# A graph network kernel with another prologue: loads in order of use, groups' columns side by side, small groups' second products turned, graph 0's norm and sums beside layer 0

## The chip, the cores and the metric

The kernel runs on one core of a Trainium2 chip. The metric is the device time of one execution in microseconds (us). Three runs of the kernel before took 2833.07, 2834.61 and 2835.61 us; the median is 2834.61.

## The reference

Four layers run one after another over 16 graphs of 1024 nodes with 256 features each; after each layer the input is added and the row is normalised (mean and variance over the 256 features). `A` is a dense 1024 x 1024 adjacency per graph.

```python
x = layernorm(x + L0(x, adj))     # layer 0: only the first 25 nodes of a graph
x = layernorm(x + L1(x, adj))     # layer 1: attention, z = x W^T + bW, softmax(leaky(ai + aj^T) masked by adj > 0) @ z
x = layernorm(x + L2(x, adj))     # layer 2: relu(((1 + eps) x + adj @ x) @ W1 + b1) @ W2 + b2
x = layernorm(x + L3(x, adj))     # layer 3: silu(rmsnorm((eps x + adj @ x) @ W1 + b1) * w) @ W2 + b2

# layer 0, for five groups of nodes: all 25; 0-8; 0 and 9-14; 6-8 and 12-14; 3-5 and 9-11
A = adj_g + I;  d = rowsum(A) ** -0.5;  N = d[:, None] * A * d[None, :]
h   = relu(N @ (x_g @ W1[g]) + b1[g])          # 256 -> 512
o_g = relu(N @ (h   @ W2[g]) + b2[g])          # 512 -> 256
fused[group] += softmax(fusion_w)[g] * o_g
```

Only the first 25 rows of each graph are changed by layer 0 before its norm; the other rows are normalised as they come in.

## The kernel before

The program has two blocks. **prologue** makes everything that all graphs share, and layer 0 of all 16 graphs; **layers** then runs layers 1 to 3 graph by graph. Each block gives every engine a queue written out by hand: `sp` (SyncE, loads and stores), `act` (ScalarE), `pool` (GpSimd), `dve` (VectorE) and `pe` (TensorE). An engine works its queue in order and waits on semaphores (`wait_ge`); the next block begins when all engines have left the one before. In the profile, SPq and ACTq are the issues of loads on the queues of SyncE and ScalarE.

**Prologue.** Four graphs of 32 padded rows fill the 128 partitions, so layer 0 has T0 = 4 tiles of rows. SP waits for two memsets, then issues 32 small loads (L155 and L157: for each graph the 25 x 25 corner of the adjacency into `A0` and 25 rows into `X0`), then the group weights `G1` and `G2` (L158, L159) and the weights of layers 2 and 3 (L160 to L163). ScalarE issues W_nat (L174) and 16 small columns and rows (L177, L195). VectorE waits for all 15 columns, builds the row mask and a zeroed copy of A, waits for the 32 loads, adds the identity (L278), copies the groups' blocks (L282), sums rows (L285); POOL raises them to -1/2 (L244); VectorE scales A (L292). It then waits for all five weights and splits W12, W13 and W23 into a high and a low part (L297, L298), so that fp32 products can be made of three faster ones. TensorE begins only when all weights and columns are there (L370, then L376, L382, L388), then transposes A (L395, five banks); VectorE scales these into `AT` (L333). TensorE multiplies x with A's columns: for each group, half of the features, tile and run of nodes one product (L410, 64 of them, 4 to 100 columns wide), and VectorE copies each bank to `XaT` (L338). In the profile an fp32 product is recorded as two instructions, a transpose as one.

For each group g, `hidden(g)` makes x A W1 (L427, eight products), ScalarE adds the bias and takes the relu into `H1` (L213, one instruction a run of nodes, four graphs' rows padded to 32). Then the second product takes H1 as weights, four tiles of 128 padded rows by G2 (L442, 16 products of 256 columns), VectorE copies to `Z` (L344), TensorE multiplies by AT (L447, four products), VectorE adds the bias (L349), ScalarE takes the relu scaled by the fusion weight (L227), POOL adds it to X0 (L250). The group's steps follow one another; only hidden(g + 1) is made ahead. At the end SP waits for all additions, stores the 16 graphs' 25 rows to `x_l0` (L168), and waits for the stores.

**Layers.** `load_x` (L620 to L623) and `load_row` (L626) bring graph 0's x and adjacency. VectorE takes statistics (L1347, L1351, L1355), POOL the inverse root (L1177), VectorE normalises (L1362) and makes two weighted sums of each row (`attention_sums`, L1370) that give `ai` and `aj` (L1376, L1377). TensorE spreads aj along rows (L732); VectorE and ScalarE make scores, mask, maximum and exponential (L1383, L1012, L1389, L1394, L1017). Then `turn_att` (L705) transposes the attention, two banks for a tile of 1024 columns; ScalarE casts each bank to the high part (L965), VectorE makes the low part (L1301) and so frees the bank. All eight tiles are turned, and then the aggregation of layer 1, first half of the columns, runs (`agg_step`, L754, L755, L758: six products of 512 columns per step, eight steps). Each step frees a tile of the adjacency's columns for a load (L644). For later graphs all this is woven into the graph before. `graph(b, first)` on TensorE then turns the adjacency's columns (`turn_col`, L719): in the first graph six of them ahead of the second half of the aggregation, the others by `COL_AT` between its steps. The rest of a graph (layers 2 and 3) is the same for every graph.

```python
for k in range(NT):                       # TensorE, graph 0, before
    turn_att(0, k)
...
for k in range(6):
    turn_col(b, k, 0)
for k in range(NT):
    agg_step(b, 1, k, 1)
    if k in COL_AT:
        turn_col(b, *COL_AT[k])
    if k == 2:
        attention_out(b, 0, first)
```

## Time and profile before

| | us |
|---|---|
| median of 3 runs | 2834.61 |
| lowest and highest | 2833.07, 2835.61 |
| profiled execution, its own time | 2838.37 |
| its span, first to last instruction | 2836.6 |
| TensorE busy (matmul) | 2685.7 (95%) |
| VectorE busy | 2027.3 (71%) |
| ScalarE busy | 1561.6 (55%) |
| POOL busy | 1273.3 (45%) |
| mean granted TensorE clock | 0.98 of full speed |

### The profile page before, as it was taken

What the parts mean: (1) busy time and instruction counts of PE and PEld (TensorE: products, weight loads), DVE (VectorE), ACT (ScalarE), POOL (GpSimd) and SP (SyncE); (2) the same over time, 40 slices, a digit from 0 to 9 for tenths busy, and PEclk for the clock granted to TensorE, in tenths of its full rate; (3) what the DMA queues carried; (4) which work ended last, traced back from release to release, by engine and by line L of the source; (5) the groups of instructions that cost most, each with busy time, mean ns of one, the idle gap of its engine ahead of it and who ended that gap; (6) DMA issues with size and microseconds to landing.
All of it is one profiled execution on the core that took longest, in us unless ns stands there. A gap on an engine that the chain in (4) does not pass through costs nothing.

```text
span 2836.6 us, 41497 instructions
## 1 busy us (share of the span) xinstructions
PE 2685.7 (95%) x14794; PEld 2292.9 (81%) x14794; DVE 2027.3 (71%) x4517; ACT 1561.6 (55%) x2900; POOL 1273.3 (45%) x1392
## 2 busy tenths in 40 slices
PE   3928999999999999999999999999999999999997
PEld 3717888888888888888888888888888888888886
DVE  4256687786868678686868778686867868686735
ACT  0233665756475665656466575647556565746624
POOL 1113455453545455354545545354555535454532
PEclk9959999999999999999999999999999999999999
DMA  4024030220404021130403022040402113040200
GB/s 144 1 80 134 1 119 31 70 79 8 142 1 149 1 86 64 32 118 1 149 1 118 32 72 78 7 143 1 149 1 86 64 32 118 1 149 1 75 1 15
DMA packets 205501, 181.06 MB, mean 64 GB/s; under 512 B 17616, under 2 KB 186992, under 8 KB 205296
## 3 DMA queue, kind: packets, MB, share of 16 engines
q1 hardware_dynamic: 197728, 177.06, 19.4%
q10 hardware_dynamic: 7568, 1.34, 0.3%
q8 instruction: 119, 1.95, 0.3%
q14 instruction: 86, 0.70, 0.1%
HBM read 161.17 MB, written 17.19 MB: 63 GB/s over the span
## 4 chain that ended last, share of the span: by engine, by line
PE 67%; DVE 15%; ACT 7%; issue 3%; POOL 1%; DMA 1%; SPq 0%; ACTq 0%; DVEq 0%; POOLq 0%
PE bank L754 9%; PE bank L758 9%; PE bank L755 9%; PE bank L819 8%; PE bank L804 6%; PE bank L809 6%; PE bank L805 6%; PE bank L833 5%; PE bank L705 4%; DVE stat L1347 3%; PE bank L837 3%; DVE x_odd L1362 2%; DVE x_even L1362 2%; DVE hid L1431 2%; PE bank L719 2%
## 5 line engine op out<-in xcount | busy, mean ns | idle before, releaser
L754 PE MATMUL bank<-mt_hi,x_hi 128*128 128x512 f32 x1536 | 629.1, 410 | 0.0
L758 PE MATMUL bank<-mt_hi,x_lo 128*128 128x512 f32 x1536 | 602.6, 392 | 0.0
L755 PE MATMUL bank<-mt_lo,x_hi 128*128 128x512 f32 x1536 | 599.7, 390 | 0.0
L1177 POOL TENSOR_TENSOR rstd<-ve,neg_half 128x4 f32<-128x4 f32 x128 | 164.1, 1282 | 437.0 <-DVE ve L1355 435.4
L758 PEld LDWEIGHTS bank<-mt_hi,x_lo 128*128 128x128 f32 x1536 | 288.8, 188 | 63.7
L754 PEld LDWEIGHTS bank<-mt_hi,x_hi 128*128 128x128 f32 x1536 | 289.6, 189 | 53.7 <-ACT scratch L1048 4.2
L755 PEld LDWEIGHTS bank<-mt_lo,x_hi 128*128 128x128 f32 x1536 | 290.2, 189 | 50.8
L804 PE MATMUL bank<-a_hi,W_lo 128*128 128x512 f32 x768 | 319.5, 416 | 1.7
L1415 DVE TENSOR_TENSOR sq_sum<-sq_sum,scratch 128x512 f32<-128x512 f32 x224 | 154.8, 691 | 227.3 <-ACT scratch L1048 227.3
L805 PE MATMUL bank<-a_hi,W_hi 128*128 128x512 f32 x768 | 303.3, 395 | 0.0
L976 ACT ACTIVATE mt_hi<-bank 128x512 fp32r<-128x512 f32 x256 | 153.4, 599 | 243.9 <-PE bank L719 243.9
L833 PE MATMUL bank<-W_hi,hid_hi 128*128 128x256 f32 x1024 | 260.5, 288 | 17.3 <-ACT hid_hi L1058 17.3
L1039 ACT ACTIVATE hid<-bank,b 128x512 f32<-128x512 f32 x256 | 176.4, 689 | 140.5 <-PE bank L837 83.5
L833 PE MATMUL bank<-W_lo,hid_hi 128*128 128x256 f32 x1024 | 252.4, 280 | 0.0
L1319 DVE TENSOR_TENSOR a_lo<-bank,a_hi 128x512 fp32r<-128x512 f32 x192 | 126.3, 686 | 176.3 <-ACT a_hi L993 176.2
L809 PE MATMUL bank<-a_lo,W_hi 128*128 128x512 f32 x768 | 241.7, 396 | 0.0
L1053 ACT ACTIVATE hid<-hid 128x512 f32<-128x512 f32 x256 | 161.6, 631 | 145.3 <-DVE hid L1431 143.6
L1182 POOL TENSOR_TENSOR x_lo<-x_even,x_hi 128x256 fp32r<-128x256 f32 x192 | 163.3, 866 | 154.1 <-ACT x_hi L1003 154.1
L993 ACT ACTIVATE a_hi<-bank 128x512 fp32r<-128x512 f32 x192 | 109.3, 594 | 217.2 <-PE bank L758 212.5
L819 PE MATMUL bank<-W,hid 128*128 128x256 f32 x1024 | 226.2, 379 | 0.0
L1307 DVE TENSOR_TENSOR mt_lo<-bank,mt_hi 128x512 fp32r<-128x512 f32 x256 | 173.1, 686 | 70.2 <-ACT mt_hi L976 70.2
L1182 POOL TENSOR_TENSOR x_lo<-x_odd,x_hi 128x256 fp32r<-128x256 f32 x192 | 161.9, 858 | 125.0 <-ACT x_hi L1003 125.0
(147 smaller groups left out, 6153.8 us busy)
## 6 DMA issues: line engine op xcount, KB each, us to landing
att<-in_adj SPq DMA_DIRECT2D x128, 512.0 KB, 7.8
adj_col<-in_adj SPq DMA_DIRECT2D x256, 256.0 KB, 3.0
out<-x_even SPq DMA_DIRECT2D x64, 128.0 KB, 2.9
out<-x_odd SPq DMA_DIRECT2D x64, 128.0 KB, 2.8
x_even<-in_x SPq DMA_DIRECT2D x56, 128.0 KB, 4.7
x_odd<-in_x SPq DMA_DIRECT2D x56, 128.0 KB, 3.6
G<-in_L_gnn_W SPq DMA_DIRECT2D x2, 2560.0 KB, 13.5
W_f<-in_L_gnn_W SPq DMA_DIRECT2D x1, 1024.0 KB, 9.1
```

What stands on the lines that cost most here:

```text
L754: nc.tensor.matmul(dst[:], hi, mt_hi[:, k, cols], start=k == 0, stop=False)
L755: nc.tensor.matmul(dst[:], hi, mt_lo[:, k, cols], start=False, stop=False)
L758: mm = nc.tensor.matmul(dst[:], lo, mt_hi[:, k, cols], start=False, stop=done)
L804: nc.tensor.matmul(dst, w_lo[:, d, cols], a_hi[:, d, :], start=d == 0, stop=False)
L805: nc.tensor.matmul(dst, w_hi[:, d, cols], a_hi[:, d, :], start=False, stop=False)
L809: mm = nc.tensor.matmul(dst, w_hi[:, d, cols], a_lo[:, d, :], start=False, stop=d == DT - 1)
L819: mm = nc.tensor.matmul(out_bank[t // 2][:, t % 2 * D:(t % 2 + 1) * D], src[:, t * P:(t + 1) * P], W22[:, m, :], start=(m == 0 and t % 2 = ...
L833: nc.tensor.matmul(out_bank[t // 2][:, t % 2 * D:(t % 2 + 1) * D], hi[:, t * P:(t + 1) * P], r[:, m, :], start=(m == 0 and t % 2 == 0 and ...
L1039: nc.scalar.activation(hid[:, m, :], src, ACT.Identity, bias=b13[:, m:m + 1])
L1177: nc.gpsimd.tensor_tensor(rstd[:, norm, own], ve[:, norm, own], neg_half[:, 0:4], ALU.pow)\
L1182: nc.gpsimd.tensor_tensor(x_lo[:, t, :], x_bufs[buf][:, t, :], x_hi[:, t, :].bitcast(F32), ALU.subtract).then_inc(s_x_lo, 1)
L1307: nc.vector.tensor_tensor(mt_lo[:, k, cols], turn_bank[i][:], mt_hi[:, k, cols].bitcast(F32), ALU.subtract).then_inc(s_turn_free[i], 1)
```

## The change

1. **Loads.** Layer 0's 32 small loads become eight: for each of the four positions i in a tile, one load brings the corners (or rows) of all four tiles. G1 and G2 come in two parts, group 0 first. Then follow graph 0's x straight into `x_even` (all rows but the first 25), W12, W13, W23, W22, and graph 0's eight adjacency rows into `att`. ScalarE's small loads come in order of use and have semaphores of their own, so that TensorE's first products wait for four loads, VectorE for five scalars. The raw W12, W13 and W23 lie where their low parts go.
2. **Order.** VectorE's memsets come ahead of its waits. WT's split and the scaled identities are made while POOL takes the power. W12 and W13 are split on VectorE after graph 0's statistics; W23's high part is made on ScalarE and its low part on POOL.
3. **Columns side by side.** ScalarE copies the five groups' columns of AT without padding into `AT_side` (212 columns a tile; 32 copies). Eight products of 212 columns, two to a bank, replace the 64 of L410, and four copies replace ten.
4. **Second products.** Group 0 keeps its form. For groups 1 to 4, `second_rows` takes W2's columns as weights and the unpadded hidden rows (144, 112, 96, 96 wide) as the moving side, eight products; VectorE copies them to `ZT` with padding, `second` transposes ZT back (eight transposes), VectorE copies to `Z`. Z, Ot, Or and the additions are now pairs of tiles, 512 columns. The groups overlap more: hidden(g + 2) is made before outputs(g).
5. **Graph 0.** Its statistics, norm and attention sums stand in VectorE's queue among the groups, tile 0 last, when layer 0 has been added. ai and aj are made in the prologue; the block layers starts with aj_rows. Four stores replace 16, and nothing of graph 0 is read back.
6. **First graph's turns.** Two tiles are turned ahead; tile k + 2 is turned before step k of the first aggregation. The columns are turned behind the steps of the second half (`FIRST_COL_AT`). SP's wait for the norm of graph 0 ahead of the column loads is gone.

```diff
                 sp.wait_ge(s_zero, 2)
-                for b in range(GRAPHS):
-                    t, i = b // PER, b % PER
+                for i in range(PER):
                     rows = slice(PAD * i, PAD * i + L0_NODES)
-                    sp.dma_start(A0[rows, 0, b, 0:L0_NODES],
-                                 adj[b, 0:L0_NODES, 0:L0_NODES]).then_inc(s_aload, 16)
-                    sp.dma_start(X0[rows, t, :], x[b, 0:L0_NODES, :]).then_inc(s_aload, 16)
+                    blocks = A0[rows, 0].rearrange("p (t i) j -> p t i j", i=PER)[:, :, i, 0:L0_NODES]
+                    own = adj.rearrange("(t i) n m -> i n t m", i=PER)[i]
+                    sp.dma_start(blocks, own[0:L0_NODES, :, 0:L0_NODES]).then_inc(s_aload, 16)
+                for i in range(PER):
+                    rows = slice(PAD * i, PAD * i + L0_NODES)
+                    own = x.rearrange("(t i) n d -> i n t d", i=PER)[i]
+                    sp.dma_start(X0[rows, :, :], own[0:L0_NODES]).then_inc(s_aload, 16)
...
+                for t in range(NT):
+                    sp.dma_start(att[:, t, :], adj[0, t * P:(t + 1) * P, :]).then_inc(s_att_in[t], 16)
...
+                for g in range(3):
+                    hidden_rows(g)
+                    if g == 2:
+                        act.wait_ge(s_wload, 16 * 4)
+                        nc.scalar.activation(W23_hi[:], W23[:], ACT.Copy).then_inc(s_w23, 1)
+                for g in range(NG):
+                    group_relu(g)
+                    if g + 3 < NG:
+                        hidden_rows(g + 3)
...
+                rstd_of(REST, 0)
+                pool.wait_ge(s_w23, 1)
+                nc.gpsimd.tensor_tensor(W23_lo[:], W23[:], W23_hi[:].bitcast(F32), ALU.subtract)
+                for i in range(NG * PAIRS):
                     pool.wait_ge(s_or, i + 1)
...
+                x_statistics()
+                split(W12, W12_hi, W12_lo)
+                split(W13, W13_hi, W13_lo)
+                dve.wait_ge(s_gbload, 32)
+                second(0)
+                second_rows(1)
+                x_norm(range(1, NT), 1)
+                outputs(0)
+                second(1)
+                second_rows(2)
+                attention_sums(range(1, 5), NT - 1)
+                outputs(1)
+                second(2)
+                second_rows(3)
+                attention_sums(range(5, NT), NT - 1)
+                outputs(2)
+                second(3)
+                second_rows(4)
+                outputs(3)
+                second(4)
+                outputs(4)
...
+                hidden(0)
+                hidden(1)
+                second(0)
+                second_rows(1)
                 for g in range(NG):
+                    if g + 2 < NG:
+                        hidden(g + 2)
+                    outputs(g)
                     if g + 1 < NG:
-                        h = hidden(g + 1, h)
...
+                        second(g + 1)
+                    if g + 2 < NG:
+                        second_rows(g + 2)
...
+    FIRST_COL_AT = ((0,), (1,), (2,), (3,), (4,), (5,), (6, 7), (8, 9, 10))
...
                     turned(turn_att_use(b, k))
+                    if first and k + 2 < NT:
+                        turn_att(b, k + 2)
                     agg_step(b, 1, k, 0, None if first or k else (s_sq, b * 2 * HT3))
```

## Rows read from the trace of the kernel before

**Rows 1.** Stretches: start:end and length in us, busy us by engine, clock, DMA share, GB/s.

```profile
16.60:41.70 25.10, 0.00 (x0) 0.01 (x1) 11.09 (x30) 0.39 (x2) 3.55 (x1) 1.00 0.97 351
41.70:55.30 13.60, 12.72 (x50) 11.59 (x51) 13.32 (x20) 0.00 (x0) 0.00 (x0) 1.00 0.00 1
55.30:79.40 24.10, 24.10 (x130) 24.10 (x129) 4.61 (x12) 0.00 (x0) 0.00 (x0) 0.62 0.00 1
79.40:150.30 70.90, 61.43 (x281) 49.42 (x281) 17.25 (x41) 18.87 (x52) 14.05 (x20) 0.96 0.00 1
150.30:180.40 30.10, 0.00 (x0) 0.00 (x0) 13.65 (x60) 0.00 (x0) 2.32 (x3) 0.50 0.52 188
202.65:232.50 29.85, 25.27 (x113) 19.95 (x113) 11.85 (x19) 12.36 (x25) 7.67 (x12) 0.74 0.18 54
232.50:260.50 28.00, 22.27 (x115) 18.20 (x114) 16.93 (x43) 11.84 (x29) 9.21 (x13) 0.88 0.55 176
380.00:542.00 162.00, 160.75 (x898) 137.38 (x897) 124.21 (x276) 96.35 (x179) 78.66 (x85) 1.00 0.21 66
```

**Rows 2.** Timeline, 0 to 52 us: start, length, engine, line, instruction, idle before.

```profile
15.90 0.30 SPq L157 DMA_DIRECT2D X<-in_x  x1
...
21.10 0.90 DVE L278 TENSOR_TENSOR A<-A,ident 128x128 f32<-128x128 f32 x4
...
26.21 3.55 POOL L244 TENSOR_TENSOR dtmp<-dinv,neg_half 128x20 f32<-128x20 f32 x1 [19.83 <-DVE dinv L287]
...
30.22 2.82 DVE L292 TENSOR_TENSOR A<-A,dinv 128x2560 f32<-128x2560 f32 x1
...
41.72 1.08 PE L370 MATMUL bank<-ident,W_nat 128*128 128x128 f32 x4 [41.72 <-DMA W<-in_L_gnn_W]
...
44.78 2.29 DVE L298 TENSOR_TENSOR W_lo<-W_f,W_hi 128x2048 fp32r<-128x2048 f32 x1
```

**Rows 3.** One line's instructions, L177, ScalarE's small loads: time to landing.

```profile
DMA to landing us min/median/max: 2.2/3.1/7.4
```

**Rows 4.** Groups by form, 0 to 157 us: busy us, mean ns, idle before and releaser.

```profile
L442 PE MATMUL bank<-G,H 128*128 128x256 f32 x160 | 35.4, 379 | 0.0
...
L250 POOL TENSOR_TENSOR X<-X,Or 128x256 f32<-128x256 f32 x20 | 14.1, 728 | 106.5 <-ACT Or L227 106.5
...
L427 PE MATMUL bank<-XaT,G 128*128 128x96 f32 x32 | 4.3, 278 | 2.8 <-ACT H L213 2.8
...
L213 ACT ACTIVATE H<-bank,g_b 128x48 f32<-128x48 f32 x16 | 3.6, 304 | 0.8 <-PE bank L427 0.8
```

**Rows 5.** Groups by form, 157 to 222 us, then 380 to 542 us (501 and 683 ns).

```profile
L1012 ACT ACTIVATE att<-aj_row,ai 128x1024 f32<-128x1024 f32 x8 | 9.0, 1140 | 34.2 <-DVE scratch L1383 34.2
...
L1370 DVE SCALAR_TENSOR_TENSOR sq_sum<-x_even,v_rows 128x256 f32<-128x256 f32 x16 | 6.8, 424 | 0.5
...
L1362 DVE TENSOR_SCALAR x_even<-x_even,mv,rstd 128x256 f32<-128x256 f32 x8 | 2.8, 408 | 0.1
...
L1362 DVE TENSOR_SCALAR x_even<-x_even,mv,rstd 128x256 f32<-128x256 f32 x16 | 9.9, 683 | 0.0
...
L1370 DVE SCALAR_TENSOR_TENSOR sq_sum<-x_even,v_rows 128x256 f32<-128x256 f32 x16 | 8.0, 501 | 0.5
```

**Rows 6.** Timeline, the end of layer 0 and the start of the layers.

```profile
150.38 5.52 SPq L168 DMA_DIRECT2D x_after_l<-X  x16
...
157.63 0.26 SPq L620 DMA_DIRECT2D x_even<-x_after_l  x1
...
180.44 1.97 PE L732 MATMUL bank<-ident,aj 128*128 128x128 f32 x8 [32.69 <-DVE aj L1376]
```

**Rows 7.** Timeline, graph 0's turned tiles and the first statistics of graph 1.

```profile
205.16 1.97 PE L705 MATMUL bank<-ident,att 128*128 128x128 f32 x8 [0.56 <-DVE mt_lo L1301]
...
241.96 1.41 DVE L1347 BATCH_NORM_STATS2 stat<-x_odd 128x6 f32<-128x256 f32 x4 [3.54 <-DMA x_odd<-in_x]
```

More of the change, by code:

```diff
@@ L33, in group_size @@
     return sum(n for _, n in GROUP_RUNS[g])
+GROUP_AT = [PER * sum(group_size(i) for i in range(g)) for g in range(NG + 1)]
+SIDE = GROUP_AT[NG]
+MOST = max(group_size(g) for g in range(1, NG)) * GRAPHS
 def row(ap):
@@ L50, in sem, with split @@
             return ctx.enter_context(nc.semaphore(name))
+        def split(name, shape):
+            hi = sb(name + "_hi", shape, F32R)
+            with ExitStack() as place:
+                raw = sb(name + "_raw", shape, F32, place)
+            return raw, hi, sb(name + "_lo", shape, F32R)
         ident = sb("ident", [P, P])
@@ L225, in _, with group_relu @@
+                        nc.scalar.activation(dst, src, ACT.Relu, bias=g_b1[:, g, h:h + 1]).then_inc(s_hev, 1)
+                def group_relu(g):
+                    for u in range(PAIRS):
+                        i = g * PAIRS + u
+                        act.wait_ge(s_ev, use_out(g) + u + 1)
                         if i >= 2:
@@ new lines, in second_rows @@
+                def second_rows(g):
+                    src = bank()
+                    size, at = group_size(g), 0
+                    if g == 1:
+                        dve.wait_ge(s_pad, 2)
+                    for first, run in GROUP_RUNS[g]:
+                        for d in range(DT):
+                            cols = src[:, d * MOST:d * MOST + GRAPHS * size].rearrange("p (b j) -> p b j", j=size)
+                            last = nc.vector.tensor_copy(ZT[:, d, :, first:first + run], cols[:, :, at:at + run])
+                        at += run
+                    last.then_inc(s_ev, 1)
@@ L346, in _, with second, outputs @@
+                def second(g):
+                    for u in range(PAIRS):
+                        src = bank()
+                        nc.vector.tensor_copy(Z[:, 2 * u:2 * u + 2, :].rearrange("p t d -> p (t d)"), src[:])\
+                          .then_inc(s_ev, 1)
+                def outputs(g):
+                    bias = g_b2[:, g, :].rearrange("p (a d) -> p a d", a=1).to_broadcast([P, 2, D])
+                    for u in range(PAIRS):
                         src = bank()
+                        i = g * PAIRS + u
@@ L429, in hidden, with second_rows @@
                         last.then_inc(s_hmm, 1)
-                        h += 1
-                    return h
-                h = hidden(0, h)
+                def second_rows(g):
+                    size = GRAPHS * group_size(g)
+                    pe.wait_ge(s_hev, KH * (g + 1))
+                    if g == 1:
+                        pe.wait_ge(s_g2load[1], 16)
+                    dst = bank()
+                    for d in range(DT):
+                        for m in range(KH):
+                            last = nc.tensor.matmul(dst[:, d * MOST:d * MOST + size], G2[:, g, m, d * P:(d + 1) * P],
+                                                    H_few[:, g % 2, m, 0:size], start=(m == 0), stop=(m == KH - 1))
+                    last.then_inc(s_mm, 1)
@@ new lines, in outputs @@
+                def outputs(g):
+                    pe.wait_ge(s_ev, use_z(g) + PAIRS)
+                    for u in range(PAIRS):
+                        dst = bank()
+                        for i in range(2):
+                            last = nc.tensor.matmul(dst[:, i * D:(i + 1) * D], AT[:, g, 2 * u + i, :], Z[:, 2 * u + i, :],
+                                                    start=True, stop=True)
+                        last.then_inc(s_mm, 1)
+                pe.wait_ge(s_ev, USE_XA + DT * PAIRS)
@@ L950, in _ @@
             aj_rows(0, True)
-            for k in range(NT):
+            for k in range(2):
                 turn_att(0, k)
```

417 lines of the change are left out of this document (237 added, 180 removed).

## The prediction

> **What bounds the kernel now.** I read the stretches first, then the timeline, then the cost of one instruction. The stretches split the run in two [rows 1]. In a graph of the main loop (380 to 542 us) TensorE is busy for 160.75 of 162.00 us at full clock, and nothing in the change touches what it does there: these graphs should stay as they are. Everything before 260.5 is a start-up in which no engine is the bound for long: TensorE works 12.7 us of the first 55, nothing from 150.3 to 180.4, and after that only 1.97 us until 202.65 [rows 1, 6]. So the change is worth what the start-up loses. The reader should see five serial pieces. (1) The 32 small loads are issued one after another, the last at 15.90; work on block A begins at 21.10 and ends at 33.04; then TensorE's first instruction still waits for the last weight, until 41.72 [rows 2]. (2) L410, 128 records bounded by weight loads, lasts 24.1 us, mostly at half clock [rows 1]. (3) Five groups take 70.9 us, TensorE busy for 61.4 [rows 1]. (4) From 150.38 the result goes to HBM in 16 stores and comes back, and graph 0's norm and sums run alone; TensorE resumes at 180.44 [rows 6]. (5) The scores take until 202.65, then eight tiles are turned with nothing beside them, then the first graph's columns with stalls [rows 1, 7].
>
> **Part 1, loads.** Eight issues replace 32. At 0.30 us each, begun every 0.35 [rows 2], the last goes out at about 5.0 instead of 15.90. ScalarE's small loads took 2.2 to 7.4 us to land [rows 3], so the blocks are there between 7.2 and 12.4; I take 8.7, nearer the median of 3.1, since few packets are ahead. VectorE's two memsets, before 21.10 in the old order, now come ahead of its first wait. From the start of L278 to the end of L292 is 11.94 us, the pow of 3.55 on POOL included [rows 2]; WT's split and the two scaled identities fit inside that pow. The scaled A stands at 20.6 instead of 33.04, and TensorE, which now waits for W_nat and three columns only, has done its weight products. TensorE turns A at the low clock (8 such records took 1.97 us [rows 6]) and VectorE scales it: AT is whole at 26.3. Up to the last layer weight 11.1 MB are loaded; at 351 GB/s [rows 1] from 5.5 that is 37. Their first user, the split of W12, comes at 39.7: hidden, by 2.7 us; each microsecond beyond that lands on VectorE's queue, which has 2 more to spare. The 4.2 MB of graph 0's adjacency follow until about 49 and are read at 89.
>
> **Part 2, columns side by side.** ScalarE gets 32 small copies. The nearest row is 128x48 at 304 ns [rows 4], 16 of them in 3.6 us, so 0.21 to 0.23 each back to back: 6.8 us, begun with the first AT, so they end at 29.5, 3.2 after AT. Nothing covers that. Eight products of 212 columns follow. A 256-column product is two records of 0.22 at full clock (160 in 35.4 us [rows 4]), so 212 columns cost 0.36 at full and 0.71 at the low level: 5.7 us, and with the last copy 36.1. The same point was 79.8. TensorE idles before them, so I take the low level; full at once would be 2.8 less.
>
> **Part 3, the groups.** First products: group 0, eight of 400 columns, by the same scale 0.67 each, to 41.6; group 1 to 43.9. Group 0's second product keeps 32 records, 7.0, to 50.8; group 1's turned one 2.1, to 52.9. VectorE meanwhile does graph 0's statistics (3.6, to 39.7) (four tiles' bn_stats took 1.41 [rows 7]) and the splits of W12 and W13 (5.4, to 45.2; W13's difference alone was 2.29 [rows 2], its cast half of that, W12's half of both), done before the first Z at 47.5. For the small groups the other 128 records of L442, 28 us, become 64 records of about 0.13 (a 96-column record: 278 ns long, 32 in 4.3 us [rows 4]) and 32 transposes of 0.11: 12 us together, so 16 less. From there VectorE and TensorE share the pace. VectorE's queue from 53.1: ZT(1) 0.6, seven norms 2.5, outputs(0) 1.6, Z 1.4, ZT(2) 1.8 with its wait, four sums 3.7 (64.6); outputs(1), Z, ZT(3), three sums (71.1); outputs(2), Z, ZT(4) (74.8); outputs(3) and Z (78.0). A pair of 512 columns is priced at 0.69 (2.29 for 2048 [rows 2] is 1.1 ns a column, and 0.12 to start). Then TensorE's last products and two additions: 80.7. The sums lie partly on the path, some 3 us. ScalarE copies W23_hi after hidden_rows(2), 2.0 us by 1140 ns for 1024 columns [rows 5], to 57.4, and group_relu(0) is queued behind it. POOL then needs 4.5 us for W23_lo, at about 2.1 ns a column, since 128x256 took 728 ns with 0.19 to start [rows 4], with ten additions of 1.3 queued behind it; it is free at 61.9, the pairs come 7 us apart, and its last addition ends at 83.1.
>
> VectorE's sums and norms now run beside POOL's additions. The rows show what that can cost: one half of a sum took 424 ns with POOL idle and 501 in a graph of the loop, a norm 408 and 683 [rows 5]. I charge nothing for it in the sum: 14 sums at 0.08 are 1.1 us, part of the range. The Trainium skill, "SBUF — State Buffer", section "Who interferes with whom", says more: a VectorE instruction with two SBUF inputs, or in a two-port mode, and a GpSimd one exclude each other for a whole instruction. By that rule the two additions that meet the four sums (61.9 to 64.5) would delay VectorE by 2.6 us, and the sum would be 2738 instead of 2735.
>
> **Part 4, the end of layer 0.** The stores start at 83.2 instead of 150.38 [rows 6], a gain of 67.2. Four store issues and their landing are 3.2 us (16 took 5.52 to issue, and the next block began 1.7 later, at 157.63 [rows 6]). Beside them VectorE normalises tile 0 and sums it, to 85.5: hidden by the stores. TensorE starts at 86.8, 3.6 after the first store, where it was 30.06: a gain of 26.4. The load of x and 14 us of VectorE leave the path. Parts 1 to 4 together: 93.6.
>
> **Part 5, graph 0's turns.** The scores stay. Eight tiles were turned one per 2.53 us at the low level (1.97 and an idle of 0.56 [rows 7]), because ScalarE and VectorE empty the bank between; then 48 products. Together 29.85 [rows 1]. Interleaved, a step is one turn (1.97 low [rows 7], 0.87 full) and six products of 0.23 full, 0.43 low: 2.25 us at full, 4.4 at the low level. I take one low step after the first two turns, then full: products begin at 7.0 and end at 23.8, 6.0 less. Bounds: 0 if the clock stays low, 8 if it rises at once. Next, the first six columns, turned ahead of the second half before, move between its products, so VectorE's idle of 3.54 us until x_odd at 241.96 [rows 7], which held TensorE up, passes under products. But turn 7 arrives late, and the residual, statistics and norm are queued behind it on VectorE; TensorE waits for x_hi until 25, then 1.3 us for a_lo, where the stretch was 28.0 [rows 1]. I take 1.5 gained, bounds -2 and 5. SP loses its wait for the norm, which was over long before.
>
> **Sum.** 93.6 + 6.0 + 1.5 = 101.1, less 1.5 for some low clock in the groups, 99.6. The profiled execution took 2838.37 us (span 2836.60), 3.8 above the median of 2834.61; the difference is taken from the median: **2735 us**. A measurement can tell about 0.2%, 5.7 us, from no change.
>
> **Rivals.** (a) The loads land no earlier: fewer issues, the same packets. Then A is ready 12.4 us later: 2747. For: A's rows are 100 bytes, and g_b2 and the bias rows share the engines. Against: the old stretch was paced by issues of 0.30 us [rows 2]. Chance 0.08. (b) TensorE stays at 1.2 GHz in the groups: first products +7.2, 16 second products +6.8, the small groups +8: 22 us, 2757. For: 0.62 of full in 55.3 to 79.4 with small products [rows 1]. Against: 0.96 in the old groups, gaps and all [rows 1]. Chance 0.07. The Trainium skill, "TensorE: Matmul & The Clock Gate", Part 1, makes the clock follow recent activity; by it the waits for VectorE's norms and sums could bring (b) about. (c) Interleaving the turns brings nothing, since turn, cast and difference stay one chain and the clock is low: 2742. Chance 0.15. (d) More overlap: full clock in part 2 (-2.8), loads at 7.2 (-1.5), turns at 8, columns at 5: 2725. Chance 0.10. (e) Slower than before: att, x_even, sq_sum and the weights lie elsewhere in SBUF; if place changed an instruction's time, every graph would pay. It decides from 6.2 us a graph (99.6 / 16), 3.8% of 162; at 7 the time is 2847. Against: products fed from many places all run at one pace, TensorE 160.75 busy of 162.00 [rows 1]. Chance 0.01. (f) What TensorE saves in the groups VectorE takes up: the norms, sums and splits it did not have there (about 20 us) lie wholly on the path: 2755. Chance 0.05. The forecast keeps 0.54, the rule on the port within it.
>
> **Numbers.** The range, 2723 to 2751, holds the forecast, (a), (c) and (d), and leaves out (b), (e), (f) and a little of each end. Faster by over 0.2% 0.985, within 0.005, slower 0.01, which is (e).
>
> **What would show it.** The first aj transposes at 87 instead of 180.4; A scaled by 21; eight products of 212 columns from 30 on; x_odd's statistics without VectorE's idle of 3.54 us; aj_row's neighbours, the scores, unchanged at 22 us. It is wrong if the stores start after 90, if VectorE waits for weights before W12's split, or if a graph of the loop takes other than 162.0.

## The result and the profile after

The kernel after takes 2747.93 us (median) against 2835.11 for the kernel before on the same chip: a ratio of 0.9691, 95% interval 0.9672 to 0.9710. Of its four executions one, of 12435.71 us, was disturbed; the other three took 2746.20, 2747.20 and 2748.65. The forecast was 2735 with a range of 2723 to 2751. The profiled execution took 2746.20 (span 2744.4), 92.2 less than the profiled one of before.

First the stretches of the kernel after, cut where its own stages end; the last row is a piece of the main loop.

```profile
core 0: us, PE busy (x) PEld busy (x) DVE busy (x) ACT busy (x) POOL busy (x), PEclk, DMA share, GB/s
0.00:13.40 13.40, 8.21 (x30) 7.43 (x30) 3.12 (x13) 0.00 (x0) 4.79 (x12) 1.00 0.59 116
13.40:35.10 21.70, 4.53 (x20) 4.13 (x20) 14.15 (x33) 4.05 (x23) 3.55 (x1) 0.97 1.11 306
35.10:42.40 7.30, 5.17 (x16) 4.66 (x16) 2.41 (x5) 1.43 (x14) 0.00 (x0) 0.61 1.04 351
42.40:59.70 17.30, 17.05 (x83) 13.48 (x84) 9.99 (x22) 3.84 (x8) 1.48 (x1) 1.00 0.70 269
59.70:92.40 32.70, 24.02 (x168) 21.54 (x166) 27.57 (x68) 12.50 (x23) 17.32 (x11) 0.99 0.00 1
92.40:98.00 5.60, 0.05 (x1) 0.08 (x2) 2.46 (x11) 0.00 (x0) 0.56 (x1) 0.50 0.22 73
98.00:120.10 22.10, 1.88 (x8) 1.49 (x9) 17.39 (x35) 17.82 (x26) 0.00 (x0) 0.50 0.00 0
120.10:143.50 23.40, 22.17 (x112) 18.62 (x113) 11.55 (x19) 11.86 (x25) 7.54 (x12) 0.80 0.23 69
143.50:168.70 25.20, 19.84 (x117) 16.54 (x117) 15.29 (x41) 11.03 (x26) 7.75 (x11) 0.97 0.89 283
380.00:541.90 161.90, 160.85 (x897) 137.93 (x896) 124.12 (x277) 96.27 (x179) 78.92 (x86) 1.00 0.21 66
```

Read it against [rows 1]. The groups are done at 92.4 instead of 150.4. The scores (98.0 to 120.1) take as long as before, with the clock at its lower level, and the two halves of the first aggregation 23.4 and 25.2 us instead of 29.85 and 28.0. TensorE is busy for 17.05 of the first 17.30 us of the groups, then for only 24.02 of 32.70, VectorE for 27.57. Where the loads run, from 13.4 to 42.4, the DMA engines have no idle time left (share over 1).

The second view is the timeline of the kernel after, all engines, where something is late. ACTq and SPq are issues of loads; the second number is the time that an issue or instruction held its queue.

```profile
6.46 10.32 ACTq L240 DMA_DIRECT2D g_b<-in_L_gnn_b  x1
12.20 11.36 SPq L210 DMA_DIRECT2D x_even<-in_x  x1
12.88 0.16 DVE L355 TENSOR_REDUCE fus_m<-fus 128x1 f32<-128x5 f32 x1 [8.84 <-DMA eps_col<-in_L_gnn_epsilon]
22.58 2.83 DVE L396 TENSOR_TENSOR A<-A,dinv 128x2560 f32<-128x2560 f32 x1
28.77 0.94 ACTq L248 DMA_DIRECT2D b_row<-in_L_gnn_b  x2
31.46 0.16 DVE L403 RECIPROCAL fus_r<-fus_s 128x1 f32<-128x1 f32 x1 [5.39 <-ACT fus_e L251]
32.01 3.07 DVE L451 TENSOR_TENSOR AT<-bank,dinv 128x512 f32<-128x512 f32 x5
48.22 0.69 DVE L410 CAST W_hi<-W_raw 128x1024 fp32r<-128x1024 f32 x1 [2.44 <-DMA W<-in_L_gnn_W]
57.72 0.69 DVE L475 COPY Z<-bank 128x512 f32<-128x512 f32 x1 [2.69 <-PE bank L620]
63.93 4.53 POOL L328 TENSOR_TENSOR W_lo<-W_raw,W_hi 128x2048 fp32r<-128x2048 f32 x1 [16.59 <-ACT W_hi L299]
66.58 2.16 DVE L442 SCALAR_TENSOR_TENSOR sq_sum<-x_even,v_rows 128x256 f32<-128x256 f32 x1
68.42 2.87 POOL L335 TENSOR_TENSOR X<-X,Or 128x512 f32<-128x512 f32 x2
69.83 1.46 POOL L335 TENSOR_TENSOR X<-X,Or 128x512 f32<-128x512 f32 x1
68.78 1.36 DVE L442 SCALAR_TENSOR_TENSOR sq_sum<-x_even,v_rows 128x256 f32<-128x256 f32 x1
70.19 1.38 DVE L442 SCALAR_TENSOR_TENSOR sq_sum<-x_even,v_rows 128x256 f32<-128x256 f32 x1
71.61 0.42 DVE L442 SCALAR_TENSOR_TENSOR sq_sum<-x_even,v_rows 128x256 f32<-128x256 f32 x1
92.41 1.76 SPq L223 DMA_DIRECT2D x_after_l<-X  x4
97.95 1.94 PE L923 MATMUL bank<-ident,aj 128*128 128x128 f32 x8 [8.81 <-PEq L194]
167.32 1.09 PE L910 MATMUL bank<-ident,adj_col 128*128 128x128 f32 x4 [3.59 <-DVE mt_lo L1498]
196.84 1.03 PE L923 MATMUL bank<-ident,aj 128*128 128x128 f32 x8
```

Three things stand out. VectorE waited 8.84 us for the five scalars, then 5.39 us more for the exponential of the fusion weights, and that stood behind ScalarE's own load issues until 29.7 and a table load of 1.28: one of the issues (g_b2, 640 KB) held the queue for 10.32 us. In the kernel before the same issue took 0.46 us, and the exponential ran at 17.80 (timeline of the kernel before):

```profile
17.80 0.30 ACT L199 ACTIVATE fus_e<-fus,fus_m 128x5 f32<-128x5 f32 x1 [5.50 <-DVE fus_m L265]
```

In the kernel after, the first sum of graph 0 ends at 68.74, 0.28 us after POOL's W23_lo; the second and third (70.14, 71.57) end 0.28 us behind POOL's two additions, the second of which begins at 69.83 and ends at 71.29; the fourth has its 0.42 us again. And aj_rows comes 5.5 us after the first store.

I use the start of aj_rows in a graph as a milestone. Before it lay at 180.44 [rows 6] for graph 0 and 286.60 for graph 1, after at 97.95 and 196.84. Here are graph 1's and graph 15's, timeline of the kernel before:

```profile
286.60 1.03 PE L732 MATMUL bank<-ident,aj 128*128 128x128 f32 x8
2556.59 1.03 PE L732 MATMUL bank<-ident,aj 128*128 128x128 f32 x8
```

In the kernel after graph 15's starts at 2464.05. So the 92.2 us of the two profiled executions come in three parts: 82.5 up to aj_rows, 7.3 from there to graph 1's (106.16 against 98.89), and 2.8 in 14 graphs of the loop (162.14 against 161.94 us each); 0.3 is lost at the end.

### The profile page after: what moved, and what is told of

The parts are those of the page before. It is cut to its first block, busy times and chain, and to the rows that moved or that the text cites. A ratio compares the mean times of both kernels' runs of the same rounds, so it can differ in the third digit from the quotient of the medians.

```text
span 2744.4 us, 41122 instructions
## 1 busy us (share of the span) xinstructions
PE 2644.1 (96%) x14650; PEld 2267.5 (83%) x14650; DVE 2022.4 (74%) x4504; ACT 1561.2 (57%) x2911; POOL 1277.7 (47%) x1384
## 4 chain that ended last, share of the span: by engine, by line
PE 89%; ACT 3%; DVE 3%; issue 1%; POOL 0%; ACTq 0%; POOLq 0%; DVEq 0%
PE bank L945 13%; PE bank L949 13%; PE bank L946 12%; PE bank L1024 9%; PE bank L1010 8%; PE bank L995 6%; PE bank L996 6%; PE bank L1000 6%; PE bank L1028 4%; PE bank L910 4%; PE bank L896 4%; PE bank L975 3%; PE bank L1042 1%; ACT att L1205 1%; PE bank L923 1%
```

## The experiments

Twelve kernels ran, all made from the kernel after unless it is said otherwise. "aj0" and "aj1" are the starts of aj_rows for graphs 0 and 1.

| kernel | median us | ratio to before, 95% interval | aj0 | aj1 |
|---|---|---|---|---|
| after | 2747.93 | 0.9672 to 0.9710 | 97.95 | 196.84 |
| turns undone | 2753.44 | 0.9694 to 0.9719 | 96.95 | 203.18 |
| products by runs | 2767.81 | 0.9748 to 0.9779 | 117.57 | 216.28 |
| second products not turned | 2758.73 | 0.9717 to 0.9745 | 112.30 | 209.07 |
| small loads | 2744.59 | 0.9664 to 0.9696 | 96.50 | 194.88 |
| loads off ScalarE | 2740.57 | 0.9647 to 0.9675 | 93.68 | 192.05 |
| the same, own waits | 2742.42 | 0.9660 to 0.9689 | 93.27 | 192.32 |
| W23 on VectorE | 2742.70 | 0.9656 to 0.9681 | 94.60 | 192.89 |
| W23 late | 2744.03 | 0.9665 to 0.9694 | 95.08 | 195.21 |
| sums last | 2745.86 | 0.9671 to 0.9700 | 98.41 | 195.40 |
| together | 2730.74 | 0.9620 to 0.9647 | 84.63 | 181.45 |
| together, small loads | 2735.78 | 0.9639 to 0.9666 | 88.14 | 186.66 |
| before, placed as after | 2834.76 | 0.9984 to 1.0001 | 181.31 | 289.90 |

Two profiles of the same prologue ("after" and "turns undone") differ by 1.0 us at aj0; smaller differences there I don't read. From aj0 to aj1 the scatter is larger: two profiles of the same work took 106.16 us (before) and 108.59 (before, placed as after).

**Parts of the change undone, one at a time.** First part 6, the turns:

```diff
-                    if first and k + 2 < NT:
-                        turn_att(b, k + 2)
...
+                else:
+                    for k in range(6):
+                        turn_col(b, k, 0)
...
-            for k in range(2):
+            for k in range(NT):
                 turn_att(0, k)
```

> Only part 6 is undone: all eight tiles of graph 0's attention are turned ahead of its aggregation, the first six columns ahead of the second half, as before the change. Theory (the turns hide behind products): from the start of the first aj mask (T0) to step_2(0) the kernel after took 48.6 us and the kernel before 57.7, so this one takes about 57.5 and the run about 2757 us; the stretch up to the scores stays at 120.1. Rival (c) of the prediction (nothing in the interleaving, the 9 us came from elsewhere, such as the clock being up earlier because less idle time lies ahead of it): the stretch stays at about 49 to 51 and the run at 2748 to 2750.

From aj0 to aj1 it took 106.23 us, the kernel before 106.16 and the kernel after 98.89, so this pair gives 7.3 us for the interleaving. All kernels with it took 96.8 to 100.1 there, the three without it 106.2 to 108.6: rival (c) is out, and the size is known to some 2 us. The run rose by only 5.5, since its prologue was 1.0 us quicker and its 14 graphs of the loop 0.8.

Then the columns side by side (the 64 products of the kernel before, and ten copies straight into Xa):

```diff
-                pe.wait_ge(s_side, NG)
-                for d in range(DT):
-                    for u in range(PAIRS):
...
+                for g in range(NG):
+                    for d in range(DT):
                         dst = bank()
...
+                                    cols[:, t * PER:(t + 1) * PER, at:at + run], X0[:, t, d * P:(d + 1) * P],
+                                    AT[:, g, t, :].rearrange("p (b j) -> p b j", j=PAD)[:, :, first:first + run],
```

> Only the columns side by side are undone: no side copies, and the 64 products of 4 to 100 columns with ten copies in place of eight products and four copies. Theory (the prediction's term: 24.1 us as before against 9.8 planned, 7.3 in the kernel after from AT to the last copy): products begin with AT's first tile at about 33, the last copy of Xa ends at 56 to 58 instead of 42.4, and the run takes 2760 to 2764. Rival (the products run at full clock here, 0.2 us each, 13 us): last copy at 47, 2752.

Timeline of that kernel, VectorE, AT and the last copy of Xa:

```profile
32.05 3.07 DVE L436 TENSOR_TENSOR AT<-bank,dinv 128x512 f32<-128x512 f32 x5
60.37 0.26 DVE L441 COPY Xa<-bank 128x96 f32<-128x96 f32 x1 [3.15 <-PE bank L566]
```

Xa is whole at 60.6 instead of 42.4, 18.2 us later, and aj0 comes 19.6 later. The theory's mechanism held and its size was too small: the granted clock was 0.50 from 35 to 55 us, and the products ran from 32.88 to 60.3, some 27 us, where they had taken 24.1 in the kernel before, at a mean clock of 0.62 [rows 1]. The time, 2767.81 us, lies above the 2764 of the theory.

And the turning of the small groups' second products:

```diff
...
-                            if g == 0:
-                                for m in range(KH):
...
-                                    last = nc.tensor.transpose(dst[:, i * D + d * P:i * D + (d + 1) * P], own, ident[:])
...
+                            for m in range(KH):
+                                rows = (H_all, H_odd)[g % 2][:, m, t * PER:(t + 1) * PER, :].rearrange("p b j -> p (b j)")
+                                last = nc.tensor.matmul(dst[:, i * D:(i + 1) * D], rows, G2[:, g, m, :],
+                                                        start=(m == 0), stop=(m == KH - 1))
```

> Only the turning of the small groups' second products is undone: groups 1 to 4 take padded hidden rows as weights like group 0 (16 products of 256 columns, two records each, in place of eight narrow products and eight transposes a group); all else, pairs and graph 0's work among the groups too, as in the kernel after. Theory (the prediction's term, 16 us, TensorE sets the pace of the groups): the stores start at 106 to 110 instead of 92.4 and the run takes 2761 to 2765. Rival (VectorE's statistics, norm, sums and additions fill the groups, so TensorE's saving is mostly covered, rival (f)): 8 us or less, 2756 or less.

The stores started at 106.79 and aj0 lay at 112.30, both 14.4 later than in the kernel after. TensorE sets the pace of this kernel's groups (busy for 41.54 of the 46.8 us from 60.0 to 106.8, VectorE for 20.87), and the 14.4 us that the turned form saves are not covered by another engine; the prediction had 16. The run, 2758.73 us, stayed under the 2761 of the theory, since from aj0 to aj1 this kernel was 2.1 us quicker; see the last section.

**The loads.** Back to 32 small ones:

```diff
-                for i in range(PER):
...
+                for b in range(GRAPHS):
+                    t, i = b // PER, b % PER
+                    rows = slice(PAD * i, PAD * i + L0_NODES)
+                    sp.dma_start(A0[rows, 0, b, 0:L0_NODES],
+                                 adj[b, 0:L0_NODES, 0:L0_NODES]).then_inc(s_aload, 16)
+                    sp.dma_start(X0[rows, t, :], x[b, 0:L0_NODES, :]).then_inc(s_aload, 16)
```

> Only part 1's merging of loads is undone: 32 small loads of layer 0 instead of eight, all else as in the kernel after. Theory (issue pace): the last of them goes out 8.4 us later (24 more issues of 0.35), the work on block A starts at 17 to 19 instead of 13.45, and the big loads behind them land later too; aj_rows comes 3 to 8 us later and the run takes 2751 to 2756. Rival (a) of the prediction (the packets, not the issues, set when the blocks are there): A's work starts within 1 us of 13.45 and the run takes 2748.

Neither theory. Block A's work did start 3.9 us later, when the last block of x had landed (the last of the 32 loads was issued at 13.47), but the run was no slower. The timeline of this kernel shows why:

```profile
5.87 3.09 ACTq L237 DMA_DIRECT2D g_b<-in_L_gnn_b  x1
15.98 0.30 ACT L248 ACTIVATE fus_e<-fus,fus_m 128x5 f32<-128x5 f32 x1
17.37 0.90 DVE L360 TENSOR_TENSOR A<-A,ident 128x128 f32<-128x128 f32 x4 [7.17 <-DMA X<-in_x]
30.53 0.69 DVE L448 TENSOR_TENSOR AT<-bank,dinv 128x512 f32<-128x512 f32 x1
```

With SyncE's large loads 8 us behind, g_b2's issue held ScalarE for 3.09 us instead of 10.32, and the exponential ran at 15.98 instead of 31.04. AT's first tile came 1.5 us earlier than in the kernel after although A was later. So in the kernel after it was the exponential, and not A, that set when AT began. That is tested by moving g_b1, g_b2 and the six bias loads to SyncE:

```diff
-                    act.dma_start(g_b1[:], L0_b1.rearrange("g (t p) -> p g t", p=P)).then_inc(s_gbload, 16)
...
+                    sp.dma_start(g_b1[:], L0_b1.rearrange("g (t p) -> p g t", p=P)).then_inc(s_gbload, 16)
```

> The group biases (g_b1, g_b2) and the six bias loads are issued by SyncE instead of ScalarE. Theory: the exponential of the fusion weights stood behind these issues on ScalarE's queue and held AT for 5.39 us; now AT is whole at about 30.5 instead of 35.1 and the side copies end at about 32 instead of 36.5. But VectorE still waits for the last of the four layer weights (48.2) before it splits W12, so the first Z stays at about 54 and the run at 2748, at most 1 us less. Rival 1: the 4.6 us go through to the end, 2743.5. Rival 2: the stall of the issue moves to SyncE's queue with the loads (10 us for g_b2) and all later loads come later: the split starts after 52 and the run takes 2752 or more.

Rival 1 was right (VectorE's first ZT copy, of group 1, is called ZT(1)). Timeline of this kernel:

```profile
14.28 0.30 ACT L253 ACTIVATE fus_e<-fus,fus_m 128x5 f32<-128x5 f32 x1 [7.75 <-DVE fus_m L359]
27.74 0.69 DVE L453 TENSOR_TENSOR AT<-bank,dinv 128x512 f32<-128x512 f32 x1
47.95 0.69 DVE L412 CAST W_hi<-W_raw 128x1024 fp32r<-128x1024 f32 x1 [4.76 <-DMA W<-in_L_gnn_W]
55.35 0.52 DVE L470 COPY ZT<-bank 128x144 f32<-128x144 f32 x2 [0.79 <-PE bank L605]
```

AT's start moved by 4.3 us, ZT(1) by 4.3 (from 59.67), and so did aj0; the profiled span fell by 5.0, the median by 7.4. My theory had W22's landing hold the first Z; but in the kernel after it was TensorE that VectorE waited for there (0.69 us for the first Z, 2.69 for the second at 57.72), and here the splits end just before TensorE is done. Would a semaphore for each weight give more?

```diff
-                def split(f, hi, lo):
-                    dve.wait_ge(s_wload, 16 * 4)
+                def split(f, hi, lo, own):
+                    dve.wait_ge(s_wl[own], 16)
```

> The loads are issued by SyncE as in the run before (2740.6 us), and each layer weight has a semaphore of its own: VectorE's split of W12 waits for W12 alone, no longer for W22, the last. Theory (there VectorE stood 4.76 us for W22, and the first Z followed the splits without idle time): the split starts at W12's landing, 43 to 45 instead of 47.95, W13's may wait again; the first Z comes 2 to 3 us earlier, and so does aj_rows (91 instead of 93.7): 2738. Rival (TensorE would have needed the time anyway, as in the kernel after, where Z waited for TensorE): less than 1 us, 2740.

The rival: W12's split now starts at 42.61 without a wait, the first Z is copied at 49.68, and then VectorE waits for TensorE:

```profile
42.61 0.68 DVE L413 CAST W_hi<-W_raw 128x1024 fp32r<-128x1024 f32 x1
49.68 0.69 DVE L478 COPY Z<-bank 128x512 f32<-128x512 f32 x1 [1.66 <-PE bank L623]
53.06 0.69 DVE L478 COPY Z<-bank 128x512 f32<-128x512 f32 x1 [2.69 <-PE bank L623]
55.02 0.53 DVE L471 COPY ZT<-bank 128x144 f32<-128x144 f32 x2 [1.27 <-PE bank L606]
```

Against the run before, ZT(1) is 0.3 us earlier, aj0 0.4, and the median is not lower. Up to there group 0's second product is the path.

**POOL beside VectorE.** W23 split on VectorE behind W13, nothing of it on ScalarE and POOL:

```diff
                 split(W13, W13_hi, W13_lo)
+                split(W23, W23_hi, W23_lo)
```

> W23 is split on VectorE behind W13 instead of on ScalarE (high) and POOL (low, 4.5 us). Theory (POOL's and VectorE's two-input instructions on SBUF exclude each other): the first three attention sums, 2.16, 1.36 and 1.38 us beside W23_lo, fall to 0.42 each unless one of POOL's additions lies beside them; this saves 3 to 4 us, the splits cost VectorE 3.4 more ahead of the first Z, POOL is free for the additions 4.5 us earlier: 2746 to 2749 in all. Rival (the sums are long for another reason: their first reads of x_even, or their own semaphore): they stay at 2.16, 1.36, 1.38, and the run takes 2751.

Timeline of this kernel, the first and the ninth sum:

```profile
66.42 0.85 DVE L437 SCALAR_TENSOR_TENSOR sq_sum<-x_even,v_rows 128x256 f32<-128x256 f32 x1
73.46 1.45 DVE L437 SCALAR_TENSOR_TENSOR sq_sum<-x_even,v_rows 128x256 f32<-128x256 f32 x1
```

The first three take 1.69 us together instead of 4.90 (the second and third 0.42 each). The ninth, beside an addition as in the kernel after (1.44 us there), stays long. The run was better than expected (5.2 us instead of 2 at most): the 3.5 us of the split fell mostly into time in which VectorE had waited for TensorE, so that ZT(1) came only 0.6 us later, at 60.29.

W23's high part behind the last relu, its low part on POOL beside the scores:

```diff
-                    if g == 2:
-                        act.wait_ge(s_wload, 16 * 4)
-                        nc.scalar.activation(W23_hi[:], W23[:], ACT.Copy).then_inc(s_w23, 1)
...
-                nc.gpsimd.tensor_tensor(W23_lo[:], W23[:], W23_hi[:].bitcast(F32), ALU.subtract)
...
+            nc.gpsimd.tensor_tensor(W23_lo[:], W23[:], W23_hi[:].bitcast(F32), ALU.subtract)
             for t in range(NT):
                 x_low(0, 0, t, 0)
```

> W23's high part is made by ScalarE behind the last group's relu, its low part by POOL at the start of the block layers, beside the scores; nothing else moves. Theory (the port: POOL's W23_lo of 4.53 us and the additions it delayed held VectorE's sums): the first three sums fall from 2.16, 1.36 and 1.38 us to 0.42 to 0.85, the stores start 3 to 4.5 us earlier than at 92.4, and the run takes 2743 to 2745. Rival (the gain of the run with W23 on VectorE came from elsewhere, so the port costs only what the sums show, and TensorE takes the rest back): stores at 91 or later, 2747. A cost is possible too: W23_lo beside the scores may lengthen one of VectorE's two-input instructions there by up to 4 us; then the scores take over 23 us.

The stores start at 89.54, 2.9 us earlier, and so does aj0. From ZT(1) to the first store it took 29.12 us instead of 32.74: 3.62 less, where the first three sums of the kernel after had been 3.64 longer than 0.42 each. What the exclusion took there lay on the path in full. The warned cost came too: the scores took 23.9 us instead of 22.2. Timeline of this kernel:

```profile
95.06 4.50 POOL L1473 TENSOR_TENSOR W_lo<-W_raw,W_hi 128x2048 fp32r<-128x2048 f32 x1 [3.97 <-POOLq L194]
97.66 2.45 DVE L1572 TENSOR_SCALAR scratch<-att 128x1024 f32<-128x1024 f32 x1
102.79 0.69 DVE L1572 TENSOR_SCALAR scratch<-att 128x1024 f32<-128x1024 f32 x1
```

The first mask of the scores, 0.69 us when alone, took 2.45 and ended at 100.11, 0.55 behind POOL's instruction. It has one input in SBUF: such an instruction is hit as well.

All 14 sums behind the last group:

```diff
-                attention_sums(range(1, 5), NT - 1)
...
-                attention_sums(range(5, NT), NT - 1)
...
                 outputs(4)
+                attention_sums(range(1, NT), NT - 1)
```

> The 14 attention sums of tiles 1 to 7 stand behind the last group's additions in VectorE's queue instead of among the groups. Theory (VectorE sets the pace of the groups, and the sums, about 7.4 us and some 5 us of exclusion by POOL, lie wholly on it, as rival (f) has it): the stores start at 81 to 83 instead of 92.4, then sums and tile 0's norm (11 us) decide, and aj_rows comes at 92 to 95 instead of 97.95: 2743 to 2745. Rival (TensorE sets the pace and the sums were mostly hidden): the stores start at 88 or later and aj_rows at 98 or later: 2749 or more.

The stores started at 89.16, aj0 lay at 98.41: the rival, and with it rival (f) of the prediction is out. The run, 2745.86 us, was quicker than the rival's 2749, because from aj0 to aj1 it took 1.9 us less (last section). Taking 7 us of sums and 4.7 of exclusion from the groups saves 3.3 us up to the stores, 4.1 counted from ZT(1). W23 late saved 2.9 and 3.6 with the sums left in place. So the sums themselves cost some 0.4 us, which is within the scatter, and the exclusion nearly all of it.

**The main loop's 0.2 us a graph.** The kernel before, with att, x_even, sq_sum and graph 0's small buffers first in the block layers:

```diff
     att = sb("att", [P, NT, NODES])
+    x_even = sb("x_even", [P, NT, D])
+    sq_sum = sb("sq_sum", [P, HALF])
...
-    x_bufs = [sb("x_even", [P, NT, D]), sb("x_odd", [P, NT, D])]
+    x_bufs = [x_even, sb("x_odd", [P, NT, D])]
```

> The kernel before, with nothing changed but the order of the buffers in SBUF: att, x_even, sq_sum and graph 0's small ones come first in layers, as in the kernel after, so mt_hi, mt_lo, x_hi and all behind them lie 10.5 KB further. Theory (place in SBUF changes the pace of the main loop's instructions a little): a graph of the loop takes 161.82 us instead of 162.01 and the run about 2832. Rival: the 0.19 us a graph come from something else, such as the phase in which the loop starts or one profile's scatter: 162.0 a graph and 2835.

Its timeline has graph 1's and graph 15's aj_rows at

```profile
289.90 1.03 PE L734 MATMUL bank<-ident,aj 128*128 128x128 f32 x8
2556.84 1.04 PE L734 MATMUL bank<-ident,aj 128*128 128x128 f32 x8
```

which is 161.92 us a graph, where before took 162.14. The kernel after and the eleven made from it, all placed in that way, show 161.89 to 162.00. Single products differ too, over the 14 graphs: the 672 of `a_lo` by `W_hi` take 396 ns each in the kernel before and 391 in this one and in the kernel after, the 896 of `W_lo` by `hid_hi` 279 and 283. So place accounts for the 2.8 us, as far as one profile of each kernel can tell; which instructions carry it I did not find. The medians do not show it (the interval holds 1): in its profile this kernel was 0.9 us later at aj0 and 2.4 us longer from there to aj1, as much as the loop gave back.

**Together.** SyncE issues all loads but nine, in order of use; each weight and x have semaphores of their own; A's work waits for A's four loads alone, the scalars are taken behind the row sums; W23 is split on VectorE.

```diff
-                dve.wait_ge(s_cload, 16 * 5)
-                step(nc.vector.reduce_max(fus_m[:], fus[:], axis=AX.X))
...
-                dve.wait_ge(s_aload, 16 * 2 * PER)
+                dve.wait_ge(s_aload, 16 * PER)
...
                 nc.vector.tensor_tensor(dinv[:], deg[:], deg0[:], ALU.add).then_inc(s_deg, 1)
+                dve.wait_ge(s_cload, 16 * 5)
+                step(nc.vector.reduce_max(fus_m[:], fus[:], axis=AX.X))
```

> What the earlier runs point to, put together on the kernel after: ScalarE issues only W_nat, the attention columns and the five scalars; SyncE issues the rest in order of use (group 0's W1, its bias, x, then W12, W13, the later groups' W2, W23, g_b2, W22); each layer weight and x have semaphores of their own; VectorE starts on block A when the four loads of A are there and takes the five scalars behind the row sums; W23 is split on VectorE. Theory: A's work begins at 8 to 10 us instead of 13.45 (the prediction's 8.7), AT is whole at 26 to 28 instead of 35.1, aj_rows starts at 84 to 88 instead of 97.95, and the run takes 2732 to 2736 us. Rival (the loads are bound by packets, so A lands no earlier than 13, or x and group 0's weights come late): aj_rows at 90 or later, 2738 to 2740.

```profile
7.75 0.90 DVE L364 TENSOR_TENSOR A<-A,ident 128x128 f32<-128x128 f32 x4 [3.71 <-DMA A<-in_adj]
24.32 0.69 DVE L456 TENSOR_TENSOR AT<-bank,dinv 128x512 f32<-128x512 f32 x1 [0.16 <-PE bank L571]
79.09 1.15 SPq L244 DMA_DIRECT2D x_after_l<-X  x3
```

This timeline is close to what the prediction had planned: A's work at 7.75 (planned 8.7), AT whole at 25.0 (26.3), stores at 79.1 (83.2). The run, 2730.74 us, where the theory had 2732 to 2736, is 0.6% faster than the kernel after and 3.7% faster than before. Last, the 32 small loads in this kernel, by the edit shown above (x's loads counted on their own semaphore):

> The kernel of the combined run (2730.7 us) with one thing put back: 32 small loads of layer 0 instead of eight. In the kernel after, putting them back cost nothing (2744.6 against 2747.9): block A was ready 3.9 us later, but AT waited for ScalarE's exponential until 31.5 either way. Theory (the merged loads gain what their issues save as soon as nothing else holds AT): A's work starts at 16 to 17 instead of 7.75, AT is whole at 33 to 34 instead of 25.0, aj_rows comes at 91 to 94 instead of 84.6, and the run takes 2737 to 2740. Rival (another cover remains, the landing of x or of the weights, so the loads are worth nothing here too): aj_rows within 2 us of 84.6, 2731 to 2733.

A's work starts at 14.18, AT is whole at 31.4, aj0 lies at 88.14, and the run is 5.0 us slower. Merging the loads is worth 3.5 us at aj0 here and nothing in the kernel after. The other 1.7 us lie between aj0 and aj1 (98.52 against 96.82), where the work is the same and the clock rose later (mean 0.52 against 0.80, last section); no run ties that to the loads. The size at aj0 was below my theory because A's loads alone were in at 14.18, where the small-loads run had waited for A and x until 17.37.

## Why the prediction was right, and where it was off

The direction, the stages and most sizes held; the time came out 12.9 us above the forecast, inside the range. Of these, 7.4 lie in the profiled executions (99.6 forecast, 92.2 measured) and 5.5 in the step from profile to median: the profiled execution of before was 3.8 above its median, that of after 1.7 below.

Two of the three signs that I had named for being wrong came: VectorE waited for weights before W12's split, and the stores started at 92.4, after 90; the third, a graph of the loop other than 162.0, by 0.06 us only. At aj_rows the kernel was 11.1 us behind the plan (97.95 against 86.8). AT was whole 8.8 us late; part 2 won back 2.5 (7.3 us from AT to the last copy, 9.8 planned); from there to the first store it took 50.0 us instead of 47.1; and part 4 was 1.9 longer. That only 7.4 us of it are left in the whole is partly luck: 1.5 had been allowed for a low clock in the groups, which did not come, and 2.8 came from the loop, which no term foresaw. Point by point:

- **Part 1** was forecast to scale A by 20.6 and have AT whole at 26.3; it was 25.4 and 35.1. The step "the blocks are there at 8.7" took care of A's packets but not of the wait ahead of them in VectorE's queue: eps_col landed 8.0 us after its issue, where I had 2.2 to 7.4 for such loads [rows 3] and applied it to A alone. And AT stands in VectorE's queue behind the exponential, as it did before; but ScalarE's issues now ran into full DMA engines. I priced the issues of SyncE and none of ScalarE's. The merging of 32 loads into eight, which I took as the source of the gain, gained nothing in this kernel, as the small-loads run shows: with 32 loads AT's first tile still came at 30.53, where TensorE had not begun until 41.72 in the kernel before [rows 2]. The order of the waits did that, as the run with the loads off ScalarE and the combined one bear out.
- **Weights** were forecast to land at 37 and to be hidden by 2.7 us. The last landed at 48.2. I had taken 351 GB/s for all from 5.5 on; it was 159 from 5.5 to 13.4 and 306 from 13.4 to 35.1 (of the 16141 packets up to 50 us, 7457 were under 512 B), and from 37.83 on the adjacency's rows were loaded beside the last weight. VectorE waited 2.44 us for them. It cost nothing that shows: TensorE was later still.
- **Part 2** was under-priced as a gain. The 32 side copies ran in 3.81 us instead of 6.8 and ended 1.4 after AT, the products took 5.17, most of it at the low clock (5.7 forecast). Undoing it costs 19.6 us at aj_rows, where my difference was 24.1 less 9.8.
- **Part 3**: apart from the port, the plan of the groups held. The turned form is worth 14.4 us against 16. The norms took 2.34 (2.5), the sums 0.42 each when alone.
- **The port.** I charged nothing for sums beside POOL and gave 2738 for the rule. The sums lost 4.7 us (2.16, 1.36, 1.38 and 1.44 against 0.42). The Trainium skill, "SBUF — State Buffer", section "Who interferes with whom", states that the two exclude each other for a whole instruction, and the trace agrees: the ends at 68.74, 70.14 and 71.57 lie 0.28 us behind POOL's. What I worked out by it, 2.6 us, was low because W23_lo started late, at 63.93, and met the first sum too.
- **Part 4**: 5.5 us from store to aj_rows instead of 3.6. Issues shrank from 5.52 to 1.76 as planned. But behind the last issue SyncE waited 3.3 us for the landing, where it had waited 1.2 behind 16 small stores, and my 3.6 was built on the old step of 1.7 to the next block.
- **Part 5**: 7.3 against 7.5, but two misses cancel in it. The first half took 23.4 against 23.8, and the second half 25.2 where I had 26.5, so the two gained 9.2; the rest up to graph 1's aj_rows then took 28.1 us instead of 26.1. Its mean clock was 0.91, where the kernel before had 1.00: it was at its lower level from 168 to 172, after TensorE had been busy for only 0.7 of the 4 us before. The stall at turn 7 was where it was foretold (3.59 us at 167.32).
- **The loop** was taken as unchanged at 162.0. It gained 0.2 us a graph, by place as far as the runs show. Rival (e) had the mechanism and the wrong sign, at a thirtieth of the size from which it decides. Rival (b) did not come: the clock was 0.99 to 1.00 from 42.4 to 92.4.

## What to carry to other kernels

A load's issue is an instruction of its engine's queue, and it can hold it for 10 us when the DMA engines are behind; keep loads that nobody needs soon off a queue that has work, and price both issue queues. When several things are ready at about the same time, undoing one shows nothing; clear the last of them first, then measure the others again. Before placing work in an idle engine, look at what POOL runs in that window: here VectorE's sums and the mask of the scores, which work from SBUF to SBUF, ended only 0.28 to 0.55 us behind POOL's instruction. Its copies out of TensorE's banks did not wait: two of 512 columns took 1.28 us beside W23_lo (at 64.05), as they did with POOL idle in the run with W23 on VectorE (at 59.09).

## What the runs showed of the hardware that I had not expected

- Issues of loads that take 0.3 to 0.5 us when the DMA engines are free took 10.32 (g_b2, 640 KB, on ScalarE), 11.36 (x_even, 896 KB, on SyncE) and 5.58 (W12, 512 KB, on SyncE) in the kernel after, between 6.5 and 32.5 us, where the DMA share was 0.80 and then over 1. In the run with the loads off ScalarE the x_even issue took 0.44 us, behind a g_b2 issue that had held the same queue, so the time is not the load's own.
- A graph of the main loop took 162.14 us in the kernel before and 161.89 to 162.00 in the 13 kernels with other places in SBUF, one profile each; one of the 13 differs from before by place alone.
- After the scores, with the same work, the granted clock rose at different times. In the 9.4 us that begin 22.1 us after aj_rows its mean was 0.50 to 0.54 in the kernel after and six others with the turns interleaved, and 0.79 to 0.81 with the sums last, with the second products not turned, and in the combined kernel. These three took 96.8 to 97.0 us from aj0 to aj1, those seven 98.3 to 99.1 (W23 late is left out, since its scores were longer). Why it rose earlier there is open. The kernel after, then the combined one:

```profile
120.05:129.45 9.40, 8.12 (x30) 6.57 (x31) 5.11 (x9) 4.84 (x11) 2.93 (x4) 0.50 0.01 2
106.73:116.13 9.40, 7.80 (x43) 6.49 (x44) 5.47 (x10) 5.90 (x14) 2.93 (x4) 0.80 0.04 11
```
